# Weights, thresholds and row statistics of a ternary feed-forward stage, taken into the last batch of the attention stage before it

## The chip, the cores and the metric

One core of a Trainium2 chip runs the whole program. The metric is device time in microseconds (us) of that core, from the first to the last instruction; lower is better. The engines named below are PE (TensorE, matrix products), ACT (ScalarE), DVE (VectorE), POOL (GpSimd) and SP (SyncE, which issues the transfers). Each works through its own instructions in program order and waits on semaphores for the others.

## The reference, cut to what matters

Eight layers change a residual `x` of 4 x 512 rows of 512 numbers, four attentions and four feed-forwards in turn. The change lies at the passage from the fifth (attention, one head 512 wide) to the sixth (ternary feed-forward):

```python
x = x + _L2_attn_ref(_layernorm(x, axis=-1), ...)   # q, k with rotary turn, softmax(q k^T) v, output weight
x = x + _L2_ffn_ref(_layernorm(x, axis=-1), L2_ffn_w_fc, L2_ffn_w_proj)

def absmax_quant(x):
    gamma = jnp.max(jnp.abs(x), axis=-1, keepdims=True)
    x_hat = jnp.clip(x * Q_B / gamma, -Q_B + EPS, Q_B - EPS)
    return x_hat * gamma / Q_B
def ternarize_weights(w):
    gamma = jnp.mean(jnp.abs(w))
    return jnp.sign(jnp.round(w / (gamma + EPS))) * gamma
def bitlinear(x, w):
    xn = layer_norm(x)
    return jnp.einsum('bsd,od->bso', absmax_quant(xn), ternarize_weights(w))
h = gelu(bitlinear(x, w_fc))        # 512 -> 2048
return bitlinear(h, w_proj)         # 2048 -> 512
```

No number of the ternary first weight is known before the mean of all its magnitudes is, and no row can be turned before its mean and variance are.

## The kernel before

`build` calls the eight stages one after the other. Each stage is a block: five engine programs that start together and join at a barrier at the end, which every engine must reach before any starts the next block. The residual stays in on-chip memory (`x`, 16 tiles of 128 rows, `NT` = 16, four tiles a batch, `TT` = 4, four batches, `NB` = 4). Each stage lays its buffers over those of the stage before, from `prog.stage_at` on.

`attention512` works through a hand-written list `ORDER` of jobs (kind, batch, number), which every engine follows for its own part: `T` turns a tile of normalised rows, `qk` makes a 128-wide piece of q or k, `U` multiplies the turned rows with the joined value and output weight, `S` makes the scores of a tile of queries, `PT` turns its exponentials, and `PV` is the product that is added to `x`. `BANK` names the PSUM bank of each job.

- DVE takes row maxima (`S`, L1608), splits values into a high and a low part (`U` L1600, `PT` L1616), and adds to `x` (`PV`, L1627). In the last batch (`b + 1 == NB`), which has no next batch to prepare, it also calls `tiles_ahead` behind its first three `S` jobs: statistics of the twelve tiles of batches 0 to 2 for the next stage.
- ACT makes the exponentials and the high parts.
- POOL adds the output bias to the four tiles of a batch (L1462), prepares the next batch's inverse roots (L1440, L1442), and computes a share of a table for the last stage of the program: `TableShare` runs 31 steps a batch (16 compare-and-scale steps, L335 and L340, and 15 additions, L345), spread over the `S`, `PT` and `PV` jobs.
- SP runs `table_moves`: it fetches indices, waits for the 31 steps of a part, stores the finished part (L320), and at the end waits until the last store has landed (L323). Only then does it come to the barrier.

`ternary_feed_forward` then starts with everything: SP issues the eight transfers of the two weights (1 MB each). DVE takes the statistics of the last four tiles, POOL the inverse roots of all 16 (`roots`, L253 to L262, two of the seven steps a power), ACT the magnitudes of the four parts of the first weight. From then on:

- `row` (DVE, L1856 to L1863) normalises and clips a tile, `turn` (PE, L1975) turns it, `turned` (ACT) and `turned_rest` (DVE) split it.
- `total_of(0)` and `threshold(0)` sum the magnitudes and make the threshold; `beneath` (ACT, a sign and a relu pass) and `ternary` (DVE, L1895 and L1898) make each weight part ternary. `inner(0)` (PE, L1991) multiplies tile 0 with part after part as they come.
- `spread` (DVE, L1907 and L1911) takes the statistics of the hidden rows, POOL four small steps on them (L1773 to L1780), `centre` (ACT, L1816) and `clipped` (DVE, L1916 to L1920) normalise and clip them, and only then can `turn_hidden` (PE, L2001) go on. DVE also makes the second weight's four parts ternary here, two of them with ACT's `beneath`.

## Time and profile before

| What | Value |
|---|---|
| runs (3) | 3374.14, 3376.9, 3380.0 us; median 3376.9 |
| profiled execution, first to last instruction | 3376.4 us |
| mean granted TensorE clock over it | 0.936 |
| busy share of the span: PE, DVE, ACT, POOL | 89%, 59%, 46%, 30% |
| first products of the last attention batch's `S`, and the last `PV` product's end | 1949.8 us and 1975.5 us |
| first product of the ternary stage | 2002.6 us |
| matmuls of the ternary stage's tiles from 2060 on: PE busy in 2060 to 2100 | 35.1 of 40 us |

No time of its own is listed for the profiled execution beside its span; it lies 0.5 us under the median of the runs. A time inside the program is counted from the span's start. In the rows further down a timeline row reads: start, us of busy time, engine, line, operation, result <- sources, shapes, count; in brackets the idle time ahead of it and what ended it. `x4` with one time is four instructions merged.

### The profile page before, as it was taken

The page shows a single profiled execution, that of the slowest core. Times are in us where ns is not written, and L with a number is a line of the kernel's source. Part 1 is how long each engine was busy: PE and PEld are TensorE (multiplying, and loading weights), DVE is VectorE, ACT ScalarE, POOL GpSimd, SP SyncE. Part 2 cuts the span into 40 slices and gives each one's busy share as a digit, 9 for nine tenths or more (in the row PEclk, how much of TensorE's full clock was granted, in tenths as well). Part 3 has the DMA queues.
Part 4 walks back from the last instruction along what each step waited for, and adds up shares of the span by engine and source line. Part 5 has one row for each costly group of instructions (what it writes and reads, how often), then busy time and mean ns, then how long its engine had stood idle before and what let it go on. Part 6 is the DMA issues. An engine that isn't in the chain of part 4 may idle for free. (4 is left out here: it accounts for less than half of the span.)

```text
span 3376.4 us, 46857 instructions
## 1 busy us (share of the span) xinstructions
PE 2992.2 (89%) x16388; PEld 2260.9 (67%) x16388; DVE 1996.1 (59%) x5348; ACT 1551.2 (46%) x3598; POOL 1019.2 (30%) x1143
## 2 busy tenths in 40 slices
PE   6999799997999977978788767998689999989999
PEld 4777678885666645446566646775467777768887
DVE  5666587775555554233747767664678777742121
ACT  5777566664666652133222244444455555531000
POOL 3655333222444530000156640000133233322222
PEclk9999899998999987988899988999799999999999
DMA  2000301101000021203100020003100000020000
GB/s 87 2 2 1 113 32 32 32 32 63 1 2 1 2 67 64 100 7 117 66 4 4 2 101 1 1 1 119 34 1 1 1 1 1 1 103 13 13 13 13
DMA packets 65872, 105.51 MB, mean 31 GB/s; under 512 B 9315, under 2 KB 29795, under 8 KB 65509
## 3 DMA queue, kind: packets, MB, share of 16 engines
q1 hardware_dynamic: 65222, 102.41, 8.7%
q8 instruction: 132, 2.16, 0.3%
q14 instruction: 102, 0.84, 0.1%
q0 software_dynamic: 416, 0.10, 0.0%
HBM read 89.75 MB, written 12.85 MB: 30 GB/s over the span
## 5 line engine op out<-in xcount | busy, mean ns | idle before, releaser
L714 POOL TENSOR_SCALAR a_P<-a_P,a_rec 128x512 f32<-128x512 f32 (+3 forms) x256 | 301.5, 1190 | 350.9 <-DVE a_rec L872 350.9
L402 ACT ACTIVATE tree_value<-tree_bit,table_lut,tree_step 128x256 f32<-128x256 uint8 x496 | 275.3, 595 | 140.8 <-DVE tree_value L416 73.0
L416 DVE COPY_PREDICATED tree_value<-tree_bit,tree_value 128x256 f32<-128x256 uint8 x434 | 235.0, 547 | 133.3 <-ACT tree_value L402 104.9
L787 ACT ACTIVATE a_P<-a_P,a_low 128x384 f32<-128x384 f32 (+3 forms) x512 | 281.7, 558 | 25.0 <-DVE a_low L866 24.9
L101 PE MATMUL bank<-f_xT_hi,f_w_hi 128*128 128x512 f32 (+1 forms) x704 | 276.6, 393 | 14.0 <-DVE f_w_lo L1214 14.0
L102 PE MATMUL bank<-f_xT_hi,f_w_lo 128*128 128x512 f32 (+1 forms) x704 | 276.1, 392 | 0.0
L103 PE MATMUL bank<-f_xT_lo,f_w_hi 128*128 128x512 f32 (+1 forms) x704 | 275.7, 392 | 0.0
L1136 POOL CAST f_h_hi<-f_sg 128x512 fp32r<-128x512 f32 (+1 forms) x88 | 84.5, 961 | 587.6 <-DVE f_sg L1236 297.8
L866 DVE CUSTOM_DVE_ANT_0 a_P<-bank,a_causal 128x384 f32<-128x384 f32 (+3 forms) x512 | 222.9, 482 | 63.1 <-PE bank L949 62.6
L794 ACT ACTIVATE a_PT<-bank 128x512 f32<-128x512 f32 x320 | 174.2, 594 | 83.3 <-PE bank L960 82.6
L1236 DVE TENSOR_TENSOR f_sg<-bank,f_sg 128x512 f32<-128x512 f32 (+1 forms) x44 | 30.4, 691 | 269.4 <-PE bank L103 269.4
L960 PE MATMUL bank<-ident,a_P 128*128 128x128 f32 x1280 | 181.2, 287 | 9.2 <-issue 6.0
L960 PEld LDWEIGHTS bank<-ident,a_P 128*128 128x128 f32 x1280 | 148.9, 146 | 40.6 <-issue 30.0
L2342 ACT ACTIVATE a_PT<-bank 128x512 f32<-128x512 f32 x112 | 61.7, 595 | 220.6 <-PE bank L2615 220.6
L1172 ACT ACTIVATE f_sg<-bank 128x512 f32<-128x512 f32 (+1 forms) x44 | 26.3, 598 | 296.3 <-PE bank L103 296.2
L101 PEld LDWEIGHTS bank<-f_xT_hi,f_w_hi 128*128 128x128 f32 (+1 forms) x704 | 132.8, 189 | 43.3 <-issue 14.4
L102 PEld LDWEIGHTS bank<-f_xT_hi,f_w_lo 128*128 128x128 f32 (+1 forms) x704 | 132.8, 189 | 28.9
L103 PEld LDWEIGHTS bank<-f_xT_lo,f_w_hi 128*128 128x128 f32 (+1 forms) x704 | 132.6, 188 | 28.9
L101 PE MATMUL bank<-f_w_hi,f_h_hi 128*128 128x512 f32 (+1 forms) x352 | 140.9, 400 | 10.2 <-POOL f_h_lo L1138 10.2
L2329 ACT ACTIVATE a_P<-bank,a_nm,a_qs 128x256 f32<-128x256 f32 (+1 forms) x256 | 134.6, 545 | 22.1 <-DVE a_nm L2479 21.9
L102 PE MATMUL bank<-f_w_hi,f_h_lo 128*128 128x512 f32 (+1 forms) x352 | 138.7, 394 | 0.0
L103 PE MATMUL bank<-f_w_lo,f_h_hi 128*128 128x512 f32 (+1 forms) x352 | 138.6, 394 | 0.0
(464 smaller groups left out, 7922.7 us busy)
## 6 DMA issues: line engine op xcount, KB each, us to landing
f_w_raw<-in_f_w SPq DMA_DIRECT2D x11, 768.0 KB, 12.8
f_w_raw<-table_w SPq DMA_DIRECT2D x11, 768.0 KB, 11.2
tree_idx<-in_f_idx SPq DMA_DIRECT2D x62, 128.0 KB, 2.1
table_w<-tree_value SPq DMA_DIRECT2D x62, 128.0 KB, 1.7
x_res<-in_x SPq DMA_DIRECT2D x4, 1024.0 KB, 10.8
m_piece<-in_m_wq SPq DMA_DIRECT2D x2, 2048.0 KB, 12.1
m_piece<-in_m_wo SPq DMA_DIRECT2D x2, 2048.0 KB, 8.5
m_piece<-in_m_w_gate SPq DMA_DIRECT2D x2, 2048.0 KB, 10.4
```

Source lines behind the costliest of these rows:

```text
L101: pe.matmul(out, w[0], x[0], start=first, stop=False, skip_group_check=True)
L102: pe.matmul(out, w[1], x[0], start=False, stop=False, skip_group_check=True)
L103: return pe.matmul(out, w[0], x[1], start=False, stop=last, skip_group_check=True)
L402: act.activation(prog.tree_value[(h + to) % 4][:, :], prog.tree_bit[h % 2][0][:, :], ACT.Identity, bias=prog.table_lut[:, 2 * k:2 * k + 1] ...
L416: dve.copy_predicated(prog.tree_value[(h + keep) % 4][:, :], prog.tree_bit[h % 2][bit][:, :], prog.tree_value[(h + other) % 4][:, :]).then ...
L714: last = pool.tensor_scalar(Pr[j][:, g, col:col + n], Pr[j][:, g, col:col + n], rec[:, j, i, g:g + 1], None, ALU.mult)
L787: last = act.activation(Pr[j][:, k, col:col + n], Pr[j][:, k, col:col + n], ACT.Exp, bias=low[:, j, i, k:k + 1], scale=-1.0, accum_out=tot ...
L794: act.activation(PT[at % NPT][:, :], ps[J.bank(key)][:, :], ACT.Copy).then_inc(J.frees(key), 1)
L866: last = dve.tensor_tensor_reduce(out=Pr[j][:, k, col:col + n], in0=ps[J.bank(source)][:, col:col + n], in1=causal[:, T - n:T], scale=-sca ...
L960: last = pe.transpose(ps[J.bank(key)][:, g * P:(g + 1) * P], Pr[j][:, g, col + kt * P:col + (kt + 1) * P], prog.ident[:, :])
L1136: pool.tensor_copy(h[i % 2][0][0:n, :], sg[i % 2][0:n, :]).then_inc(c_hi.sem, 1)
L2329: e = act.activation(Pr[i][:, hh, lo:2 * P], ps[3 + j][:, h2 * 2 * P + lo:(h2 + 1) * 2 * P], ACT.Exp, bias=small["nm"][:, i, hh:hh + 1], s ...
```

## The change

- A class `TernaryMemory` lays the ternary stage's buffers by hand, at the places that the attention's last batch has done with: the first weight over q's and k's weights, the second over the joined weight and the turned rows. The two tiles of normalised rows and their turned parts lie over buffers of the `qk` jobs. The first weight is now four parts, each in one piece.
- SP issues the eight weight transfers from inside `table_moves` (`ahead`), before it waits for the last table part.
- Statistics of tiles 0 to 7 go behind the `S` jobs of batches 1 and 2, one tile each; those of tiles 8 to 11 behind the last batch's first `U` job. `tiles_ahead` is no longer called here.
- The last batch has an `ORDER` of its own with new jobs: `size` (ACT, magnitudes of a first-weight part), `row` (DVE, normalise and clip tiles 0 and 1), `fT` (turn and split them), `gamma` (sum and threshold of the first weight), `below` (ACT, the sign and relu pass of part 1).
- POOL computes the inverse roots of tiles 0 to 11 (`ternary_roots`) when it meets the first `size`, and those of tiles 12 to 15 at the start of the ternary stage.
- In the ternary stage the magnitudes of two of the second weight's parts go from DVE to ACT, and DVE takes the last four tiles' statistics behind `row(2)`.

```diff
@@ table_moves: SP @@
     for i in range(first, last):
+        if i + 1 == last:
+            ahead()
         sp.wait_ge(*prog.table_step(0, (i + 1) * TABLE_STEPS))
...
@@ ternary_roots: POOL @@
+    pool.wait_ge(*c_mv(0, done + 1))
+    for out, a, b, op in ((var[:, 0, r], prog.mv[:, r, 1], 1e-5, ALU.add), (var[:, 1, r], var[:, 0, r], half, ALU.pow),
+                          (var[:, 2, r], var[:, 1, r], var[:, 1, r], ALU.mult), (var[:, 2, r], var[:, 2, r], prog.mv[:, r, 1], ALU.mult)):
...
+    pool.tensor_tensor(var[:, 2, r], var[:, 2, r], half, ALU.pow).then_inc(prog.count("ln_pow").sem, 1)
+    pool.wait_ge(*prog.count("ln_pow")(0, done + 1))
+    pool.tensor_tensor(prog.rstd[:, r], var[:, 1, r], var[:, 2, r], ALU.mult).then_inc(c_rstd.sem, 1)
...
@@ attention512: ORDER, behind the U jobs of a batch @@
+        if b + 1 == NB:
+            ORDER += [("size", b, 0), ("S", b, 0), ("size", b, 1), ("S", b, 1), ("PT", b, 0), ("row", b, 0), ("S", b, 2), ("size", b, 2),
+                      ("PT", b, 1), ("fT", b, 0), ("PV", b, 0), ("size", b, 3), ("S", b, 3), ("row", b, 1), ("PT", b, 2), ("gamma", b, 0),
+                      ("PV", b, 1), ("fT", b, 1), ("PT", b, 3), ("PV", b, 2), ("below", b, 0), ("PV", b, 3)]
+            break
...
@@ attention512: SP @@
+            def weights_ahead():
+                for n in range(4):
+                    sp.wait_ge(*full("qk", NB - 1, 3 if n < 2 else 7))
...
+                sp.wait_ge(*full("U", NB - 1, TT - 1))
...
+            table_moves(prog, sp, *share, weights_ahead)
@@ attention512: POOL @@
             for kind, b, k in ORDER:
+                if kind == "size" and k == 0:
+                    ternary_roots(prog, pool, slice(0, HEAD_TILES), 0)
                 if kind in ("S", "PT", "PV"):
                     table.run(pool)
...
@@ attention512: ACT @@
+                elif kind == "size":
+                    act.wait_ge(*f_in[k](0, 32))
...
+                    act.activation(M.below[0][:, :, :], M.fc_part(True, k), ACT.Abs, accum_out=M.sums[:, k:k + 1]).then_inc(f_fsum.sem, 1)
...
@@ attention512: DVE, U and S @@
+                    elif k == 0 and b + 1 == NB:
+                        for t in range(HEAD_TILES - TT, HEAD_TILES):
+                            last = dve.bn_stats(prog.stats[:, t, :], x[:, t * D:(t + 1) * D])
+                        last.then_inc(f_lnstat.sem, 1)
+                    elif k == 1 and b + 1 == NB:
+                        dve.wait_ge(*f_lnstat(0, 1))
+                        for t in range(HEAD_TILES):
+                            last = dve.bn_aggr(prog.mv[:, t, :], prog.stats[:, t, :])
+                        last.then_inc(f_lnmv.sem, 1)
...
-                    if k < 3 and b + 1 == NB:
-                        tiles_ahead(prog, dve, range(k * TT, (k + 1) * TT))
+                    if b and b + 1 < NB:
+                        t = (b - 1) * TT + k
+                        dve.bn_stats(prog.stats[:, t, :], x[:, t * D:(t + 1) * D])
...
@@ ternary_feed_forward: POOL @@
-            prog.roots(pool, 1e-5, 1e-6)
+            ternary_roots(prog, pool, slice(HEAD_TILES, NT), 1)
...
@@ ternary_feed_forward: ACT @@
-            magnitudes(0)
-            magnitudes(1)
-            turned(0)
-            turned(1)
-            magnitudes(2)
-            magnitudes(3)
-            for i in range(3):
-                beneath(i)
-            gelu(0)
+            beneath(1)
+            magnitudes(0)
+            beneath(2)
+            gelu(0, (0, 1))
+            magnitudes(1)
+            gelu(0, (2, 3))
...
@@ ternary_feed_forward: DVE @@
-            prog.statistics(dve)
-            row(0)
-            row(1)
-            turned_rest(0)
-            turned_rest(1)
+            ternary("fc", 0)
+            ternary("fc", 1)
+            magnitudes(2)
+            ternary("fc", 2)
+            magnitudes(3)
+            ternary("fc", 3)
             row(2)
-            threshold(0)
-            for n in range(4):
-                ternary("fc", n)
-            magnitudes(0)
-            magnitudes(1)
+            for t in range(HEAD_TILES, NT):
+                last = dve.bn_stats(prog.stats[:, t, :], x[:, tile(0, t)])
+            last.then_inc(c_lnstat.sem, 1)
             spread(0)
-            magnitudes(2)
-            magnitudes(3)
+            dve.wait_ge(*c_lnstat(0, 2))
+            for t in range(HEAD_TILES, NT):
+                last = dve.bn_aggr(prog.mv[:, t, :], prog.stats[:, t, :])
+            last.then_inc(c_lnmv.sem, 1)
             threshold(1)
             clipped(0)
```

How the instructions stand now, at two places. POOL in the attention's last batch, before: the bias on four tiles, then straight into the 31 table steps (`table_sum`, `table_term`).

```order
L1462 TENSOR_TENSOR x_res<-x_res,a_bo 128x512 [waits xn] x4
L335 TENSOR_SCALAR table_sum_65<-table_idx_60,table_lut 128x256 [waits table_out1,table_in1]
L340 TENSOR_SCALAR table_term_62<-table_idx_60,table_lut 128x256 [waits table_step]
L340 TENSOR_SCALAR table_term_63<-table_idx_60,table_lut 128x256 [waits table_step]
L345 TENSOR_TENSOR table_sum_65<-table_sum_65,table_term_62 128x256 [waits table_step]
```

The same place in the changed kernel (`var` and `rstd` are the inverse roots of twelve tiles, `ln_mv` is DVE's signal that their means and variances are there):

```order
L1575 TENSOR_TENSOR x_res<-x_res,a_bo 128x512 [waits xn] x4
L1419 TENSOR_SCALAR var<-mv 128x12 [waits ln_mv]
L1421 TENSOR_TENSOR var<-var,mhalf 128x12 [waits ln_var]
L1421 TENSOR_TENSOR var<-var 128x12 [waits ln_var]
L1421 TENSOR_TENSOR var<-var,mv 128x12 [waits ln_var]
L1425 TENSOR_SCALAR var<-var 128x12 [waits ln_var]
L1427 TENSOR_TENSOR var<-var,mhalf 128x12 [waits ln_var]
L1429 TENSOR_TENSOR rstd<-var 128x12 [waits ln_pow]
L337 TENSOR_SCALAR table_sum_65<-table_idx_60,table_lut 128x256 [waits table_out1,table_in1]
L342 TENSOR_SCALAR table_term_62<-table_idx_60,table_lut 128x256 [waits table_step]
```

The seven root steps, and a wait for DVE ahead of them, now stand between the bias and the batch's 31 table steps.

DVE at the start of the ternary stage in the changed kernel, from the barrier to the hidden rows' statistics (`f_fc` is the ternary first weight, `f_sums` magnitudes of second-weight parts, `f_xn` a normalised tile, `f_hstats` the statistics of the hidden rows):

```order
L2016 TENSOR_SCALAR f_below_19433<-f_raw_fc,f_gamma 128x2048
L2019 SCALAR_TENSOR_TENSOR f_fc<-f_raw_fc,f_gamma,f_below_19433 128x2048 [waits h_neg]
L2019 SCALAR_TENSOR_TENSOR f_fc<-f_raw_fc,f_gamma,f_below_19431 128x2048 [waits w_below]
L2023 TENSOR_REDUCE f_sums<-f_raw_pj 128x1 [waits w_in6]
L2019 SCALAR_TENSOR_TENSOR f_fc<-f_raw_fc,f_gamma,f_below_19432 128x2048 [waits w_below]
L2023 TENSOR_REDUCE f_sums<-f_raw_pj 128x1 [waits w_in7]
L2019 SCALAR_TENSOR_TENSOR f_fc<-f_raw_fc,f_gamma,f_below_19431 128x2048 [waits w_below]
L1389 TENSOR_SCALAR f_xn_19439<-x_res,mv,rstd 128x512
...
L1396 TENSOR_SCALAR f_xn_19439<-f_xn_19439,f_gmax 128x512 [waits clip_neg]
L2062 BN_STATS stats<-x_res 128x6 x4
L2028 BN_STATS f_hstats<-f_h_19434 128x6 [waits bank_free0]
```

The block opens with the ternary first part, where before it opened with statistics, rows and the threshold; one row and four tiles' statistics follow.

## Rows read from the trace of the kernel before

**Rows 1.** Timeline of PE across the passage between the two stages.

```profile
1989.27 1.11 PE L1975 MATMUL bank<-ident,f_xn 128*128 128x128 f32 x4 [13.77 <-DVE f_xn L1863]
...
2002.62 0.77 PE L1991 MATMUL bank<-f_fc,f_xT_hi 128*128 128x512 f32 x1 [4.57 <-issue]
```

**Rows 2.** Timeline of DVE: the attention's end, the ternary stage's first rows.

```profile
1975.54 0.75 DVE L1627 SCALAR_TENSOR_TENSOR x_res<-bank,a_rec,x_res 128x512 f32<-128x512 f32 x1 [1.97 <-PE bank L103]
1976.61 2.47 DVE L209 BATCH_NORM_STATS2 stats<-x_res 128x6 f32<-128x512 f32 x4 [0.32 <-PEq L1425]
...
1987.17 0.55 DVE L1856 TENSOR_SCALAR f_xn<-x_res,mv,rstd 128x512 f32<-128x512 f32 x1 [7.68 <-POOL rstd L262]
...
1989.13 0.54 DVE L1856 TENSOR_SCALAR f_xn<-x_res,mv,rstd 128x512 f32<-128x512 f32 x1
```

**Rows 3.** Timeline of POOL: last batch's table steps, then the roots.

```profile
1939.18 2.09 POOL L335 TENSOR_SCALAR table_sum<-table_idx,table_lut 128x256 f32<-128x256 int32 x1
...
1970.37 1.55 POOL L345 TENSOR_TENSOR table_sum<-table_sum,table_term 128x256 f32<-128x256 f32 x2
1979.59 0.27 POOL L253 TENSOR_SCALAR var<-mv 128x16 f32<-128x16 f32 x1 [7.66 <-DVE mv L213]
1979.94 2.94 POOL L257 TENSOR_TENSOR var<-var,mhalf 128x16 f32<-128x16 f32 x1
```

**Rows 4.** Waits of SP's queue, 1960 to 1980: engine, line, waited for, us.

```profile
SPq L1425 <- PEq L1425: 2.3, 1, 2.3
SPq L323 <- DMA table_w<-table_sum: 1.6, 1, 1.6
```

**Rows 5.** Timeline of DVE in the last batch: `U` parts, means and variances.

```profile
1941.65 1.28 DVE L1600 TENSOR_TENSOR a_U_lo<-bank,a_U_hi 128x512 fp32r<-128x512 f32 x2
...
1955.79 0.38 DVE L495 BATCH_NORM_AGGREGATE mv<-stats 128x2 f32<-128x6 f32 x4
```

**Rows 6.** Timeline of POOL in batch 2: roots of four tiles, 31 table steps.

```profile
1873.97 1.04 POOL L1442 TENSOR_TENSOR rstd<-var,mhalf 128x4 f32<-128x4 f32 x1
1875.01 1.17 POOL L335 TENSOR_SCALAR table_sum<-table_idx,table_lut 128x256 f32<-128x256 int32 x1
...
1887.35 1.40 POOL L340 TENSOR_SCALAR table_term<-table_idx,table_lut 128x256 f32<-128x256 int32 x1
...
1905.42 1.55 POOL L345 TENSOR_TENSOR table_sum<-table_sum,table_term 128x256 f32<-128x256 f32 x2
```

**Rows 7.** Timeline of DVE in batch 2: four normalised tiles beside those steps.

```profile
1887.29 2.62 DVE L1546 TENSOR_SCALAR a_xn<-x_res,mv,rstd 128x512 f32<-128x512 f32 x4
```

**Rows 8.** Waits of DVE in batches 1 and 2: line, waited for, us, times, longest.

```profile
DVE a_nm L1608 <- PE bank L103: 10.5, 8, 2.0
```

**Rows 9.** The last batch in one stretch: length, then busy PE, PEld, DVE, ACT, POOL, clock.

```profile
1943.00:1976.00 33.00, 30.82 (x136) 24.77 (x134) 17.63 (x42) 6.38 (x14) 26.70 (x29) 0.95 0.02 5
```

**Rows 10.** Timeline of DVE: ternary parts, magnitudes, hidden rows' statistics, first clip.

```profile
1998.85 1.29 DVE L1895 TENSOR_SCALAR f_below<-f_raw_fc,f_gamma 128x2048 f32<-128x2048 f32 x1
2000.17 2.35 DVE L1898 SCALAR_TENSOR_TENSOR f_fc<-f_raw_fc,f_gamma,f_below 128x2048 fp32r<-128x2048 f32 x1
...
2010.50 2.35 DVE L1898 SCALAR_TENSOR_TENSOR f_fc<-f_raw_fc,f_gamma,f_below 128x2048 fp32r<-128x2048 f32 x1 [1.49 <-ACT f_below L1805]
2012.77 4.47 DVE L1902 TENSOR_REDUCE f_sums<-f_raw_pj 128x1 f32<-128x2048 f32 x2
2017.16 2.46 DVE L1907 BATCH_NORM_STATS2 f_hstats<-f_h 128x6 f32<-128x512 f32 x4
...
2025.76 2.29 DVE L1916 TENSOR_REDUCE f_hmax<-f_h 128x1 f32<-128x2048 f32 x1 [0.20 <-ACT f_h L1816]
```

**Rows 11.** Timeline of POOL: the four steps on the first hidden rows' statistics.

```profile
2020.22 0.23 POOL L1773 TENSOR_SCALAR f_hvar<-f_hmv 128x1 f32<-128x1 f32 x1 [33.08 <-DVE f_hmv L1911]
...
2021.58 0.25 POOL L1780 TENSOR_SCALAR f_hshift<-f_hvar 128x1 f32<-128x1 f32 x1 [0.19 <-POOL f_hvar L1777]
```

**Rows 12.** Timeline of ACT: the first hidden rows normalised (`centre`).

```profile
2023.57 2.08 ACT L1816 ACTIVATE f_h<-f_h,f_hshift,f_hrstd 128x2048 f32<-128x2048 f32 x1
```

More of the change, by code:

```diff
@@ L303, in table_part, with table_moves @@
     return part[:, i % 2 * TABLE_COLS:(i % 2 + 1) * TABLE_COLS]
-def table_moves(prog, sp, first, last):
+def table_moves(prog, sp, first, last, ahead):
     def fetch(i):
@@ new lines, in ternary_roots @@
+def ternary_roots(prog, pool, r, done):
+    c_mv, c_var, c_rstd = prog.count("ln_mv"), prog.count("ln_var"), prog.count("ln_rstd")
+    var, half = prog.var, prog.mhalf[:, r]
+    steps = 5 * done
+    pool.wait_ge(*c_mv(0, done + 1))
+    for out, a, b, op in ((var[:, 0, r], prog.mv[:, r, 1], 1e-5, ALU.add), (var[:, 1, r], var[:, 0, r], half, ALU.pow),
+                          (var[:, 2, r], var[:, 1, r], var[:, 1, r], ALU.mult), (var[:, 2, r], var[:, 2, r], prog.mv[:, r, 1], ALU.mult)):
+        if op == ALU.add:
+            last = pool.tensor_scalar(out, a, b, None, op)
+        else:
+            last = pool.tensor_tensor(out, a, b, op)
+        steps += 1
+        last.then_inc(c_var.sem, 1)
+        pool.wait_ge(*c_var(0, steps))
+    pool.tensor_scalar(var[:, 2, r], var[:, 2, r], 1e-6, None, ALU.add).then_inc(c_var.sem, 1)
+    pool.wait_ge(*c_var(0, steps + 1))
+    pool.tensor_tensor(var[:, 2, r], var[:, 2, r], half, ALU.pow).then_inc(prog.count("ln_pow").sem, 1)
+    pool.wait_ge(*prog.count("ln_pow")(0, done + 1))
+    pool.tensor_tensor(prog.rstd[:, r], var[:, 1, r], var[:, 2, r], ALU.mult).then_inc(c_rstd.sem, 1)
@@ L1417, in attention512 @@
     c_uhi, c_max, c_pthi, c_rec = (prog.count(n) for n in ("u_hi", "row_max", "pt_hi", "rec"))
+    f_in = [prog.count(f"w_in{i}") for i in range(8)]
+    f_fsum, f_below, f_sign, f_xhi, f_xn = (prog.count(n) for n in ("w_sums", "w_below", "w_sign", "fT_hi", "xn_ready"))
+    f_gamma, f_rstd, f_lnstat, f_lnmv = (prog.count(n) for n in ("w_gamma", "ln_rstd", "ln_stats", "ln_mv"))
     NQK = len(QK)
@@ L1633, in _ @@
                 key = (kind, b, k)
-                if kind == "T":
+                if kind in ("size", "row", "below"):
+                    continue
+                if kind == "fT":
+                    pe.wait_ge(*f_xn(0, k + 1))
+                    pe.wait_ge(*vacant(*key))
+                    for c in range(DC):
+                        last = pe.transpose(bank(*key)[:, c * P:(c + 1) * P], M.xn[k][:, c * P:(c + 1) * P], prog.ident[:, :])
+                elif kind == "gamma":
+                    pe.wait_ge(*f_fsum(0, 4))
+                    pe.wait_ge(*vacant(*key))
+                    last = pe.matmul(bank(*key)[:, 0:4], prog.ones[:, :], M.sums[:, 0:4], start=True, stop=True)
+                elif kind == "T":
                     pe.wait_ge(*c_xn(0, b * TT + k + 1))
@@ L1736, in ternary_feed_forward @@
     h_norm, h_max, h_neg, h_ready, h_hi = (prog.count(n) for n in ("h_norm", "h_max", "h_neg", "h_ready", "h_hi"))
-    once = [prog.count(n) for n in ("ln_stats", "ln_mv", "ln_rstd")]
-    c_var = prog.count("ln_var")
+    c_lnstat, c_lnmv, c_rstd, c_var, c_pow = (prog.count(n) for n in ("ln_stats", "ln_mv", "ln_rstd", "ln_var", "ln_pow"))
     H_BANK = (4, 5, 6, 4)
-    jobs = [(("T", 0), 5), (("T", 1), 5), (("sum", 0), 7)] + [(("F", 0, n), n) for n in range(4)]
+    jobs = [(("F", 0, n), n) for n in range(4)]
     for t in range(NT):
@@ L1805, in beneath, with gelu @@
                 act.activation(below[i % 2][:, :, :], below[i % 2][:, :, :], ACT.Relu).then_inc(c_below.sem, 1)
-            def gelu(t):
+            def gelu(t, which=range(4)):
                 if t >= 2:
                     act.wait_ge(*full("H", t - 2, 3))
-                for n in range(4):
+                for n in which:
                     act.wait_ge(*full("F", t, n))
@@ L1990, in inner @@
                         for i in (0, 1):
-                            last = pe.matmul(ps[n][:, :], xT[t % 2][i][:, k, :], fc[:, k, n * D:(n + 1) * D], start=k == 0 and i == 0,
+                            last = pe.matmul(ps[n][:, :], xT[t % 2][i][:, k, :], fc[:, n, k, :], start=k == 0 and i == 0,
                                              stop=k == DC - 1 and i == 1)
```

168 lines of the change are left out of this document (106 added, 62 removed).

## The prediction

> **What bounds the kernel now.** I read the timeline of PE first, since PE is the busiest engine, and looked for the hole that the change aims at. Between the attention's last product at 1975.5 and the first product of the ternary stage at 2002.62, PE does only two tiles' turns: it waits 13.77 us for a normalised tile and later 4.57 us for the first ternary part [rows 1]. DVE's timeline says what fills the hole [rows 2]: its last addition to `x` ends at 1976.29, the barrier takes 0.32 us, four tiles' statistics follow, then 7.68 us of waiting for POOL's roots, then rows at 1.96 us each (1987.17 to 1989.13). Behind the hole the weight parts come at ACT's pace, 2.35 us of DVE and 1.49 us of waiting each, the last one done at 2012.85 [rows 10]. Then come magnitudes, hidden statistics, and at 2025.76 the first `clipped`.
>
> That instruction is my yardstick. All that DVE, ACT, PE and POOL do from it on is in the same order in both kernels, and it waits for the hidden rows' normalisation, so whatever moves it moves the end of the program by as much. The sum is made on the profiled execution (3376.4 us, 0.5 under the median of the runs).
>
> **POOL and the barrier, the term that decides.** In the last batch POOL runs its table steps from 1939.18 to 1971.92 (1970.37 + 1.55) without a break [rows 3], and was done 4.4 us before the attention was. The change puts roots ahead of these 31 steps, and a wait for DVE ahead of the roots. Step by step:
>
> - DVE begins the first `U` part at 1941.65 as before, 0.64 us (half of 1.28): 1942.3. Four statistics, 2.46 us by the four like ones at 2017.16 [rows 10]: 1944.75. The second `U` part, 0.64: 1945.4. Twelve aggregations at 0.095 (0.38 for four [rows 5]), 1.14: signal at 1946.5. PE does not mind: it needs that second part only for the fourth `U` product, after its third.
> - The roots of 16 tiles took 7.55 us (1979.59 to the row that they release at 1987.17). Two of the seven steps are powers, 2.94 us at 16 columns [rows 3] and 1.04 at four [rows 6]: 0.158 a column, so 2.31 at twelve. 7.55 - 2 x 0.63 = 6.3 us; with the signal's 0.1, ready at 1952.9. Upper bound: the whole 7.55.
> - The 31 steps took 31.96 us in batch 2 (1875.01 to 1906.97 [rows 6]) and 32.74 in the last batch. I take 31.96, because the longer one began beside DVE's last q and k work, which is over by now: POOL ends at 1984.9.
> - SP may store the part only then. Before, it waited 1.6 us for the landing and another 2.3 at the barrier [rows 4], which opened about 1976.4: it arrived at 1974.1, 2.2 us after POOL's last step. Now 1987.1. With the barrier's 0.32, the ternary stage begins at **1987.4**, 10.8 us later than before.
>
> **The last batch's other engines** are not what ends last. ACT gains four magnitude passes, a sign and relu pair and two copies, about 13 us (a pair is the 2.35 + 1.49 = 3.84 us of ACT's pace above, a pass taken as half of it); it was busy 6.38 of 33 us [rows 9]. Two of the passes stand between a score and what PE waits for next. DVE loses three groups of statistics and gets two rows. Walking through the order with these durations I get the last addition at about 1980. Bounds: 1976.3 with all of it hidden, 1989.1 with every added pass on the path, which would cost 2 us beyond POOL. Below 1987.1 it costs nothing.
>
> **Batches 1 and 2** get eight statistics of 0.62 us, behind row maxima. DVE waits 10.5 us in eight of these places for PE's next scores [rows 8], so I count nothing; with all of it on the path, 4.9 us. **The eight transfers** move ahead of SP's last wait. They wait for `qk` and `U`, over by 1950, and nothing is queued behind them but the table store, 35 us later. I count nothing.
>
> **The ternary stage, from its start s = 1987.4 to `clipped`**, with start-to-start distances of [rows 10]: the compare 1.32, each ternary pass 2.27, each magnitude pass 2.2. Passes of parts 0 and 1, a magnitude, part 2, a magnitude, part 3: the last begins at s + 12.5 and ends at s + 14.85. ACT's pairs for parts 2 and 3, with one magnitude pass between, need at most 3 x 3.84 = 11.5, so DVE does not wait for them. Then one row, 1.96, and four statistics, 2.4: `spread` begins at s + 19.15. From its start to POOL's first step was 3.06 us (2017.16 to 2020.22 [rows 11]); now four aggregations lie between, 0.38: s + 22.6.
>
> Here is the second price on POOL: the roots of tiles 12 to 15 stand ahead of the hidden rows' four steps. At four columns they take 7.55 - 2 x 1.90 = 3.75 us: s + 26.35. The four steps took 1.61 (2020.22 to 2021.83), so s + 27.95, and from `centre` to `clipped` it was 2.19 (2023.57 [rows 12] to 2025.76): s + 30.15. The other way to `centre`, over tile 1's products and their gelu, took 10.7 us from the last ternary part (2012.85 to 2023.57), which now gives s + 25.6. POOL comes 2.3 us later than that, so slower products up to that amount would not show.
>
> **Sum:** 1987.4 + 30.15 = 2017.55 instead of 2025.76, 8.2 us earlier. The median of the runs less this is 3376.9 - 8.2 = **3368.7 us**. Of some 17.6 us that the move would give with POOL out of the way, POOL takes 7.1 at the barrier and 2.3 behind it.
>
> **A rule against it.** In [rows 6, 7] DVE normalises four tiles beside the table steps: one POOL step takes 1.40 instead of 1.17, and the batch's 31.96 us hold that. In the last batch the two rows have four such DVE operations, so the term already has their price. The Trainium skill (SBUF — State Buffer, "Who interferes with whom") says that GpSimd and a VectorE operation of this kind take a shared port by turns, and that the later one blocks fully. By it each of the four could hold POOL for its own 0.55 us, 2.2 in all, and the sum would be nearer 3370.5; the 0.23 of the row is less than that.
>
> **Rivals.**
>
> 1. *The rows collide with POOL in full.* POOL's first step of the last batch took 2.09 us beside DVE's q and k work, 0.92 more than the 1.17 of batch 2 [rows 3, 6]. Four of these are 3.7 us, some 3.3 beyond what is in the term: 8.2 - 3.3 = 4.9 us gained, 3372.0 us, which is no change by my bound. For it: that step. Against it: the 0.23 beside just such DVE operations.
> 2. *The hole closes entirely.* Were POOL and SP no later than the batch's own end at 1980, the stage would start 7.1 us earlier: 15.3 us gained, 3361.6 us. It needs POOL's 31 steps to end by 1977.5. Against it: POOL's order is fixed, and its steps lie without gaps in [rows 3, 6]; nothing makes them shorter.
> 3. *Slower than before.* DVE's, ACT's and the transfers' added work in the last batch stretches POOL's steps one and all by the 0.92 of that first step: 28.5 us, 3397 us. The gain is gone from 9 such steps of 31, and from 17 (15.6 us) the kernel is measurably slower. For it: POOL is now on the path, so each such us counts. Against it: POOL kept its pace in batch 2 while DVE, ACT and PE worked beside it.
>
> **How the numbers follow.** A difference of 0.2%, 6.75 us, is about what a measurement of this kernel can tell from no change. Forecast as worked out, with its terms a little off: 0.71. First rival: 0.13. Second: 0.06. Third: 0.06. The remaining 0.04 is a gain of 2 to 6 us from small losses, such as the eight statistics of batches 1 and 2. The forecast's own range comes from roots at 6.3 to 7.55, table steps at 31.7 (without the 0.23) to 32.74, 0.4 either way at the barrier, 2 us if ACT's passes lie on the path, and 1.5 us of spread between the runs: 3366 to 3372.5. Since 0.71 alone is too little, the range takes in the first rival and a part of the second's side: 3363.5 to 3373.5. The forecast lies 1.45 us beyond the 0.2% line, so about a tenth of its chance falls within it: faster 0.64 + 0.06 = 0.70; the same 0.07 + 0.13 + 0.04 = 0.24; slower 0.06.
>
> **What will show it.** In the changed profile POOL's twelve-column roots should begin near 1946.5 and its last table addition end near 1985; DVE's first compare should follow near 1987.4, with DVE, PE and ACT idle from about 1980 until then and SP the last at the barrier. The first ternary product should start some 3.7 us behind that, four-column roots near 2010, and `clipped` near 2017.5. I am wrong in the main term if POOL ends before the batch's last addition, if DVE's or ACT's last work of the batch is the later one, or if the products of batches 1 and 2 have already shifted when the last batch begins.

## The result

The changed kernel takes 3362.64 us (median; runs from 3358.44 to 3365.48) beside 3377.14 us of the kernel before on the same chip: 14.5 us less. The ratio is 0.995, with a 95% interval of 0.9938 to 0.9962, which is a gain of 13 to 21 us. The forecast was 8.2 us and 3368.7 us, and its range ended at 3363.5: the direction was right, the gain nearly twice what was forecast. The profiled execution spans 3358.3 us, 18.1 us less than the one before.

Four instructions cut the program into pieces that can be compared: DVE's first `U` part of the last batch, the first product with the ternary first weight, DVE's first `clipped` (the yardstick), and the last product of the ternary stage. All times in the table are differences of their starts in the timelines, in us.

| Stretch | before | changed | changed, second profile | difference |
|---|---|---|---|---|
| program start to first `U` part | 1941.65 | 1940.40 | 1942.43 | (not touched) |
| `U` part to first product | 60.97 | 48.68 | 48.64 | -12.29 |
| first product to `clipped` | 23.14 | 26.15 | 26.13 | +3.01 |
| `clipped` to the ternary stage's last product | 293.78 | 287.99 | 288.03 | **-5.79** |

The second profile is that of the run "a_again" below. The stretches that hold the change repeat within 0.04 us in these two profiles, and within 0.3 us in a third, a_sink below, whose edit lies in another stage. The stages ahead, which no kernel here alters, do not: over the thirteen profiles of this study the first `U` part starts anywhere from 1937.5 to 1944.2. So a profile's whole span tells changes of a few us badly, and I compare stretches.

The passage that the forecast modelled, `U` part to `clipped`, gained 12.29 - 3.01 = 9.28 us. Another 5.79 us came from behind the yardstick, where the forecast had said nothing would happen. Together 15.1 us; the other 3 of the 18.1 lie in stages that the change doesn't touch (1.25 ahead, 1.8 behind).

### The profile page after: what moved, and what is told of

It reads as the page before. It is cut to its first block and busy times, and to the rows that moved or that the text cites. A ratio compares the mean times of both kernels' runs of the same rounds, so it can differ in the third digit from the quotient of the medians.

```text
span 3358.3 us, 46872 instructions
## 1 busy us (share of the span) xinstructions
PE 2978.5 (89%) x16388; PEld 2255.5 (67%) x16388; DVE 1990.4 (59%) x5346; ACT 1554.5 (46%) x3602; POOL 1020.2 (30%) x1150
## 5 line engine op out<-in xcount | busy, mean ns | idle before, releaser
L101 PE MATMUL bank<-f_xT_hi,f_w_hi 128*128 128x512 f32 (+1 forms) x704 | 275.5, 391 | 14.5 <-DVE f_w_lo L1216 14.5
```

Source lines behind the costliest of these rows:

```text
L101: pe.matmul(out, w[0], x[0], start=first, stop=False, skip_group_check=True)
```

## The profile after

POOL's timeline in the changed kernel, from the wait for DVE's means to the hidden rows' last step; it answers to [rows 3, 6, 11]:

```profile
1944.97 0.27 POOL L1419 TENSOR_SCALAR var<-mv 128x12 f32<-128x12 f32 x1 [7.02 <-DVE mv L1739]
1945.31 2.30 POOL L1421 TENSOR_TENSOR var<-var,mhalf 128x12 f32<-128x12 f32 x1
...
1951.21 1.17 POOL L337 TENSOR_SCALAR table_sum<-table_idx,table_lut 128x256 f32<-128x256 int32 x1
...
1957.37 1.19 POOL L342 TENSOR_SCALAR table_term<-table_idx,table_lut 128x256 f32<-128x256 int32 x1
1958.65 0.98 POOL L347 TENSOR_TENSOR table_sum<-table_sum,table_term 128x256 f32<-128x256 f32 x1
...
1981.58 1.52 POOL L347 TENSOR_TENSOR table_sum<-table_sum,table_term 128x256 f32<-128x256 f32 x2
2007.65 0.24 POOL L1419 TENSOR_SCALAR var<-mv 128x4 f32<-128x4 f32 x1 [24.55 <-DVE mv L2067]
...
2011.38 0.23 POOL L1909 TENSOR_SCALAR f_hvar<-f_hmv 128x1 f32<-128x1 f32 x1
...
2012.74 0.25 POOL L1916 TENSOR_SCALAR f_hshift<-f_hvar 128x1 f32<-128x1 f32 x1 [0.20 <-POOL f_hvar L1913]
```

Seven us of waiting, 6.24 us of roots, 31.89 us of table steps, done at 1983.10. The waits of SP's queue around the end of the attention (engine and line, waited for, us), which answer to [rows 4], show that SP came to the barrier last, and that nobody kept it waiting there (0.2 us):

```profile
SPq L325 <- DMA table_w<-table_sum: 1.4, 1, 1.4
SPq L1525 <- PEq L1525: 0.2, 1, 0.2
```

DVE's timeline answers to [rows 2, 5, 10]: the last batch's start, its last addition to `x`, 9.56 us of waiting at the barrier, and the ternary stage to `clipped`:

```profile
1940.40 0.68 DVE L1729 TENSOR_TENSOR a_U_lo<-bank,a_U_hi 128x512 fp32r<-128x512 f32 x1
...
1975.05 0.75 DVE L1779 SCALAR_TENSOR_TENSOR x_res<-bank,a_rec,x_res 128x512 f32<-128x512 f32 x1 [1.97 <-PE bank L103]
1985.36 1.28 DVE L2016 TENSOR_SCALAR f_below<-f_raw_fc,f_gamma 128x2048 f32<-128x2048 f32 x1 [9.56 <-PEq L1525]
...
1997.86 2.34 DVE L2019 SCALAR_TENSOR_TENSOR f_fc<-f_raw_fc,f_gamma,f_below 128x2048 fp32r<-128x2048 f32 x1
...
2004.45 2.46 DVE L2028 BATCH_NORM_STATS2 f_hstats<-f_h 128x6 f32<-128x512 f32 x4
...
2015.23 2.29 DVE L2037 TENSOR_REDUCE f_hmax<-f_h 128x1 f32<-128x2048 f32 x1 [4.19 <-ACT f_h L1951]
```

ACT's row ahead of `clipped` answers to [rows 12]; ACT waited for POOL:

```profile
2013.03 2.09 ACT L1951 ACTIVATE f_h<-f_h,f_hshift,f_hrstd 128x2048 f32<-128x2048 f32 x1 [2.14 <-POOL f_hshift L1916]
```

Where the 5.79 us came from shows in PE's timeline in the middle of the ternary stage. First the kernel before, then the changed one (start, length, what). In both the last row is the 24th product behind the first, with nothing but such products between:

```profile
2160.13 0.39 PE L1991 MATMUL bank<-f_fc,f_xT_hi 128*128 128x512 f32 x1
2160.36 0.39 PE L1991 MATMUL bank<-f_fc,f_xT_lo 128*128 128x512 f32 x1
...
2165.73 0.39 PE L2012 MATMUL bank<-f_pj,f_hT_hi 128*128 128x512 f32 x1
```

```profile
2147.03 0.39 PE L2114 MATMUL bank<-f_fc,f_xT_lo 128*128 128x512 f32 x1
2147.26 0.39 PE L2114 MATMUL bank<-f_fc,f_xT_hi 128*128 128x512 f32 x1
...
2152.47 0.39 PE L2114 MATMUL bank<-f_fc,f_xT_lo 128*128 128x512 f32 x1
```

24 products take 5.60 us before and 5.44 after: 233.3 and 226.7 ns from start to start. The mean over the stage, where the granted clock is 1.00, is 233.3 ns before, for both weights, and 227.6 ns (first weight) and 226.9 ns (second) after. From the fifth tile's first product to the stage's last one the clock is 1.00 all along. These are that stretch's rows, before and after (length, then busy time and count of PE, PEld, DVE, ACT, POOL, then the clock, and the transfers' share and rate):

```profile
2085.51:2319.53 234.02, 225.88 (x1082) 181.78 (x1081) 151.72 (x225) 93.38 (x124) 15.80 (x50) 1.00 0.00 1
```

```profile
2074.21:2303.22 229.01, 220.88 (x1082) 182.18 (x1081) 151.59 (x225) 93.41 (x124) 15.83 (x50) 1.00 0.00 1
```

The same 1082 products and turns take 5.01 us less, the greater part of the 5.79. From `clipped` to the fourth tile's first product nothing is gained (40.10 and 40.11 us). The other 0.78 us lie in the passage between, from the fourth tile's first product to the fifth's, in which PE has its lower clock for a part of the time:

```profile
2065.86:2085.51 19.65, 19.02 (x86) 15.28 (x85) 12.14 (x18) 7.54 (x11) 1.21 (x4) 0.92 0.00 1
```

```profile
2055.34:2074.21 18.87, 18.24 (x86) 14.96 (x85) 12.13 (x18) 7.54 (x11) 1.21 (x4) 0.94 0.00 1
```

Of the stage's 1024 such products 896 come behind the fourth tile's first one, where PE is the bound, so some 6 ns of each is 5.4 us. PE's work, its order and the other engines' work beside it are the same there. What differs is where the buffers lie. In both kernels the streamed weights begin at bytes 51904 and 84672 of each partition, 192 modulo 512. The turned rows that PE loads (`xT`, `hT`) began at 142080 and 170752 before, 256 modulo 512, because the two small buffers `gamma` and `sums` (64 bytes) stand ahead of them; `TernaryMemory` puts them at 199360 and 158400, 192 modulo 512. The distance was 64 and is now 0.

## Experiments

"Distance" is always the address of the loaded operand less that of the streamed one, in bytes modulo 512.

**1. The addresses alone, in the kernel before (b_addr).**

```diff
-    gamma = prog.sb(name + "_gamma", [P, 8], F32)
-    sums = prog.sb(name + "_sums", [P, 8], F32)
     below = [prog.sb(f"{name}_below{i}", [P, 4, D], F32) for i in range(3)]
...
     hshift = prog.sb(name + "_hshift", [P, 1], F32)
+    gamma = prog.sb(name + "_gamma", [P, 8], F32)
+    sums = prog.sb(name + "_sums", [P, 8], F32)
```

> The kernel before with one thing changed: the two small buffers gamma and sums (64 bytes together) are allocated behind the ternary stage's other buffers, so that the turned rows (the weights that PE loads, xT and hT) lie 64 bytes lower. Nothing is moved in time. Theory A (addresses): a float32r product of 512 columns takes 233.3 ns from start to start where the loaded and the streamed operand lie 64 bytes apart modulo 512, and 226.7 to 228 ns where they lie 0 apart, as in the changed kernel; expected: the 1024 products of the ternary stage at about 227 ns, that stage 5.5 to 6.5 us shorter, the program 3371 us instead of 3377, the ternary stage's first product and first clipped where they were. Theory L (layout of the first weight in four contiguous parts): no change, 233 ns, 3377 us. Theory T (the earlier start or other work beside the products): no change, 233 ns, 3377 us.

Measured: 3375.0 us beside 3380.0 us, ratio 0.999 (0.9979 to 1.0001): 5 us by the medians, but an interval that reaches no change. The stretches are sharper: `U` part to `clipped` 83.97 us (84.11 before), `clipped` to the last product 288.46 instead of 293.78. PE's timeline in the middle of the stage:

```profile
2160.11 0.39 PE L1991 MATMUL bank<-f_fc,f_xT_hi 128*128 128x512 f32 x1
2160.34 0.39 PE L1991 MATMUL bank<-f_fc,f_xT_lo 128*128 128x512 f32 x1
...
2165.55 0.39 PE L2012 MATMUL bank<-f_pj,f_hT_hi 128*128 128x512 f32 x1
```

5.44 us for 24, as in the changed kernel; 227.7 and 226.9 ns in the mean of the stage. Moving 64 bytes brings 5.3 of the 5.8 us, with nothing moved in time; I had expected 5.5 to 6.5. The steady stretch from the fifth tile on takes 229.01 us, exactly that of the changed kernel. The passage ahead of it takes 19.35 us at a mean clock of 0.91, where the changed kernel has 18.87 at 0.94: the missing 0.5 us goes with the clock and not with the addresses. The edit also moves `below`, `xn` and `h` by 64 bytes. In s_small, further down, these lie as in the kernel before modulo 512, and the products with `hT` are fast all the same.

**2. The layout alone (b_parts).**

```diff
-    fc = prog.sb(name + "_fc", [P, DC, 4 * D], F32R)
+    fc = prog.sb(name + "_fc", [P, 4, DC, D], F32R)
...
-    last = pe.matmul(ps[n][:, :], xT[t % 2][i][:, k, :], fc[:, k, n * D:(n + 1) * D], ...
+    last = pe.matmul(ps[n][:, :], xT[t % 2][i][:, k, :], fc[:, n, k, :], ...
```

> The kernel before with the first weight stored as four contiguous parts, as the change stores it; all addresses of buffers as before, so the operands still lie 64 bytes apart modulo 512. Theory A (addresses): 233.3 ns for both weights' products, no change. Theory L (layout): the first weight's 512 products at 227 ns, about 3 us less; the second weight's, whose layout is the same in both kernels, at 233 ns, which would leave the gain in them unexplained.

Measured: 233.3 ns for both weights, `clipped` to the last product 293.79 us, 3379.9 us in one run. The layout does nothing.

**3. The addresses undone in the changed kernel (a_shift).**

```diff
+        at += 64
         self.hT = [prog.sb(f"{name}_hT_{n}", ...
...
-        at = FLAT_AT
+        at = FLAT_AT - 64
         self.xn = [prog.sb(f"{name}_xn{i}", ...
```

> The changed kernel with its turned rows moved: xn and xT 64 bytes down (448 instead of 0 apart modulo 512 from the first weight), hT 64 bytes up (64 apart, as in the kernel before). Nothing is moved in time. Theory A (addresses): products at about 233 ns again, the ternary stage 5.5 to 6.5 us longer, the program about 3368.5 us, which is 8 to 9 us under the kernel before, the passage's gain alone. Theories L (layout) and T (time or neighbours): 227 ns as in the changed kernel, 3362.6 us.

Measured: 3366.5 us, ratio 0.9962 (0.995 to 0.9974). `U` part to `clipped` is as in the changed kernel (74.76 us, 74.83 there), `clipped` to the last product 291.67 us, 3.7 longer (5.5 to 6.5 expected). The second weight's products, at distance 64, take 233.4 ns again; the first weight's, at 448, take 229.3, which I had expected to be slow in full. PE's timeline, first weight and then second, the last row of each pair the 24th product behind its first (5.50 and 5.60 us):

```profile
2145.30 0.39 PE L2115 MATMUL bank<-f_fc,f_xT_lo 128*128 128x512 f32 x1
...
2150.80 0.39 PE L2115 MATMUL bank<-f_fc,f_xT_lo 128*128 128x512 f32 x1
2151.49 0.40 PE L2136 MATMUL bank<-f_pj,f_hT_hi 128*128 128x512 f32 x1
...
2157.09 0.40 PE L2136 MATMUL bank<-f_pj,f_hT_hi 128*128 128x512 f32 x1
```

**4. Other distances, and other places (s_small, s_moved).** Both are the kernel before with the ternary stage's buffers placed by hand. The edits in s_small, and behind them those in s_moved:

```diff
+    prog.at = near(57) + 32      # xT of even tiles; near(k) is stage_at + 2048 k
+    prog.at = near(60) + 128     # xT of odd tiles
+    prog.at = near(63) + 256     # hT
...
+    at = prog.stage_at + 64                   # first weight
+    at = prog.stage_at + 16 * D * 4 + 64      # second weight
+    prog.at = near(57) + 64
+    prog.at = near(60) + 0
+    prog.at = near(63) + 256
```

> The kernel before with the ternary stage's turned rows at other distances from the weights that are streamed past them (modulo 512; 64 before): even tiles' xT 32, odd tiles' xT 128, hT 256. If 0 alone is fast: 229 to 233.5 ns in all three. If distances of whole 128 or 256 bytes are free: 227 ns for the odd tiles, or for hT. If only the loaded operand's own place matters (192 modulo 512 fast): slow in all three.

> The kernel before with both weights of the ternary stage 64 bytes higher (256 instead of 192 modulo 512), and xT of even tiles at a distance of 0 from them, of odd tiles at 448, hT at 192. Theory A (the distance between the operands counts): even tiles' products 227 to 228 ns, odd tiles' 229 to 230, hT's about 232 ns. Rival (the loaded operand's own place counts, 192 modulo 512 fast): even tiles (at 256) 233 ns, odd tiles (at 192) 227 ns.

Measured in one run each, mean from start to start: distance 32, 233.4 ns; 128, 232.9; 256, 227.3 (s_small); 0, with both operands moved by 64, 227.4; 448, 229.2; 192, 229.0 (s_moved), the last faster than I had expected. From s_small, 24 products of even tiles (distance 32, 5.60 us) and 15 with `hT` (256, 3.40 us):

```profile
2158.78 0.40 PE L1997 MATMUL bank<-f_fc,f_xT_lo 128*128 128x512 f32 x1
...
2164.38 0.40 PE L1997 MATMUL bank<-f_fc,f_xT_lo 128*128 128x512 f32 x1
2166.47 0.39 PE L2018 MATMUL bank<-f_pj,f_hT_hi 128*128 128x512 f32 x1
...
2169.87 0.39 PE L2018 MATMUL bank<-f_pj,f_hT_lo 128*128 128x512 f32 x1
```

From s_moved, 24 products of even tiles with both operands at 256 (distance 0, 5.44 us):

```profile
2157.68 0.39 PE L1997 MATMUL bank<-f_fc,f_xT_hi 128*128 128x512 f32 x1
...
2163.12 0.39 PE L1997 MATMUL bank<-f_fc,f_xT_hi 128*128 128x512 f32 x1
```

The distance counts and not the place: both operands at 256 are as fast as both at 192. And 0 is not the only fast distance. With 64 from the kernel before, the values are 227 to 228 ns at 0 and 256, 229 at 192 and 448, 233 at 32, 64 and 128: all of it fits a distance taken modulo 256, though 320, for one, was not measured. `clipped` to the last product follows: 290.76 us (s_small) and 289.73 us (s_moved).

**5. The same in another stage (a_sink).** The window attention's float32r products lie at distances 128 and 384, in both kernels.

```diff
+    sink = prog.sb(name + "_sink", [P, 2, H], F32)
     wc, wc_raw = prog.pair(name + "_wc", [P, DC, P])
...
-    sink = prog.sb(name + "_sink", [P, 2, H], F32)
```

> The changed kernel with one thing changed in the window attention, a stage that the change does not touch: the buffer sink (128 bytes) stands ahead of that stage's weights instead of between them and its other buffers, so that loaded and streamed operands of its float32r products lie 0 apart modulo 512 (128 and 384 before). Theory A (addresses): these 1008 products go from 232.6 to about 227 ns, the stage 4 to 5.6 us shorter, the program 3357 to 3358.5 us instead of 3362.6. Rival (the distance matters only in the ternary stage's pattern of one streamed piece under two loaded ones): 232.6 ns as before, no change.

Measured: 3359.8 us, ratio 0.9942 (0.9927 to 0.9957), which overlaps the changed kernel's. PE's timeline in the window attention, the changed kernel and then a_sink, each time from one product to the eleventh behind it (2.55 and 2.50 us):

```profile
2505.47 0.39 PE L101 MATMUL bank<-a_w_hi,a_OT_hi 128*128 128x512 f32 x1
...
2508.02 0.40 PE L103 MATMUL bank<-a_w_lo,a_OT_hi 128*128 128x512 f32 x1
```

```profile
2502.57 0.40 PE L101 MATMUL bank<-a_w_hi,a_OT_hi 128*128 128x512 f32 x1
...
2505.07 0.39 PE L103 MATMUL bank<-a_w_lo,a_OT_hi 128*128 128x512 f32 x1
```

The 768 products with `OT` go from 232.6 to 227.9 ns, as the distance says; the 192 with `compT`, now also at distance 0, only from 232.2 to 231.9. These come three at a time between other kinds of products; whether that is the reason is not shown. The stage, from its first `OT` product to the first product of the next, takes 533.2 us where the changed kernel's two profiles have 534.7 and 535.0. That would be 1.5 to 1.8 us, where 4 to 5.6 had been expected; but a_hidden_first below, without this edit, shows 533.4. Over all thirteen profiles the two with this edit (a_sink, a_all) have 533.2 and 533.4, ten of the eleven without it 534.6 to 536.0. So the products' gain is shown, some 1.5 us for the stage is likely, and one for the program is not shown.

**6. POOL's order in the last batch (a_table_first).**

```diff
                 if kind == "size" and k == 0:
+                    for _ in range(3):
+                        table.run(pool)
                     ternary_roots(prog, pool, slice(0, HEAD_TILES), 0)
                 if kind in ("S", "PT", "PV"):
-                    table.run(pool)
+                    if table.n < 3 * NT:
+                        table.run(pool)
```

> The changed kernel with three of the last batch's twelve calls of the table share, 7 of its 31 steps, put on POOL ahead of the twelve-column roots, into the 7.0 us in which POOL waits for DVE there. Theory of the prediction (POOL's table steps and the store behind them are what ends last at the barrier): roots 0 to 1 us later, POOL's last table addition near 1976.5 instead of 1983.1, the ternary stage 6 to 7 us earlier, and the program as much: 3356 us instead of 3362.6. Rival (the batch's own work, ACT's passes or the weight transfers, ends just under POOL): POOL ends 6 to 7 us earlier, but the stage starts at most 3 us earlier, with another engine named at the barrier, 3360 us or more. Second rival: the rows and PE's turns wait longer for later roots, and the last addition to x moves up by as much as POOL is earlier: no change.

Measured: 3356.5 us, ratio 0.9928 (0.9913 to 0.9943). POOL's timeline and then DVE's first row of the ternary stage:

```profile
1945.10 1.15 POOL L342 TENSOR_SCALAR table_term<-table_idx,table_lut 128x256 f32<-128x256 int32 x1
1946.33 0.26 POOL L1419 TENSOR_SCALAR var<-mv 128x12 f32<-128x12 f32 x1
...
1975.58 1.52 POOL L347 TENSOR_TENSOR table_sum<-table_sum,table_term 128x256 f32<-128x256 f32 x2
1979.36 1.29 DVE L2019 TENSOR_SCALAR f_below<-f_raw_fc,f_gamma 128x2048 f32<-128x2048 f32 x1 [3.40 <-PEq L1525]
```

POOL ends at 1977.10, 6.0 us earlier, and the stage starts 6.0 us earlier; `U` part to first product is 42.82 us (48.68). POOL, with SP's store behind it, did set the start.

**7. The second price on POOL (a_hidden_first).**

```diff
-            ternary_roots(prog, pool, slice(HEAD_TILES, NT), 1)
             for t in range(NT):
...
                 pool.tensor_scalar(hshift[:, :], hvar[:, :], -1.0, None, ALU.mult).then_inc(h_rstd.sem, 1)
+                if t == 0:
+                    ternary_roots(prog, pool, slice(HEAD_TILES, NT), 1)
```

> The changed kernel with POOL's roots of tiles 12 to 15 put behind its four steps on the first hidden rows, instead of ahead of them. Theory of the prediction (the roots are a second price on POOL, 2.3 us, after which the other way to centre, over tile 1's products and gelu, ends last): POOL's hidden steps 3.7 us earlier, ACT's centre only about 2.1 us earlier, since ACT ends gelu of tile 1 2.14 us before centre in the changed profile; clipped 2.1 us earlier and the program 3360.5 us instead of 3362.6. Rival (ACT or PE hold centre anyway, or POOL's roots now collide with DVE's clipped): less than 1 us.

Measured: 3362.5 us, ratio 0.9952 (0.9935 to 0.9969), no difference that runs can tell from the changed kernel. In this profile the first `U` part came 3.8 us later than in the changed kernel's, in stages that both share, which hides the gain. The stretches show it: first product to `clipped` 23.86 us instead of 26.15. POOL's timeline and ACT's:

```profile
2011.23 0.24 POOL L1908 TENSOR_SCALAR f_hvar<-f_hmv 128x1 f32<-128x1 f32 x1 [24.41 <-DVE f_hmv L2033]
2012.93 0.24 POOL L1419 TENSOR_SCALAR var<-mv 128x4 f32<-128x4 f32 x1
2013.89 0.69 ACT L1948 ACTIVATE f_h<-bank,f_gamma 128x512 f32<-128x512 f32 x1 [1.12 <-PE bank L2115]
2014.48 2.08 ACT L1952 ACTIVATE f_h<-f_h,f_hshift,f_hrstd 128x2048 f32<-128x2048 f32 x1
```

POOL's `f_hshift` is there at 2012.9 now; ACT goes to `centre` without a wait behind its last gelu. The bound has passed to PE's products and the gelu, 2.29 us earlier.

**8. Three edits together (a_best, a_all, beside a_again).** a_best holds the edits of 6 and 7 and a third one, with which SP no longer waits at the barrier for its last store:

```diff
@@ table_moves @@
-    for i in (last - 2, last - 1):
-        sp.wait_ge(*prog.table_out[i % 2](0, 16 * (i // 2 + 1)))
+    i = last - 2
+    sp.wait_ge(*prog.table_out[i % 2](0, 16 * (i // 2 + 1)))
@@ ternary_feed_forward @@
+        @block.sync
+        def _(sp):
+            sp.wait_ge(*prog.table_out[3 % 2](0, 16 * (3 // 2 + 1)))
```

a_all has the edit of 5 as well; a_again is the changed kernel once more.

> The changed kernel with three edits on POOL and SP together: 7 table steps ahead of the twelve-column roots, the hidden rows' steps ahead of the four-column roots, and SP's wait for the landing of the last table part taken out of the attention's block and put into the ternary stage's. Theory of the prediction (POOL, then SP's store and landing, set the start of the ternary stage; roots delay the hidden rows): against the changed kernel the stage starts 5.9 us earlier by the first edit and 1.5 to 2 us by the third, since POOL's end (35.4 to 36.8 us after the last batch's first U part) is then the last thing at the barrier, close to the batch's own end (35.7 us after it); clipped comes another 2.3 us earlier by the second. In all 9.7 to 10.5 us less than the changed kernel, about 3352 us, 25 us under the kernel before. Rival (the third edit buys nothing, because POOL's or SP's last store is still waited for at the barrier, or the last attention addition is later): 8 us less, 3354.5 us.

> The kernel with the three edits, and the buffer sink of the window attention moved as well, so that this stage's operands lie 0 apart too. By the products alone (227 instead of 232.6 ns, 1008 of them) 4 to 5.6 us less than without it. By what the run with that edit alone showed (median start to start 227 ns, mean 230 to 231, no shorter stage than the spread of about 1 us between runs): 0 to 2 us less.

> The changed kernel itself, unaltered, on the chip of the two versions above, so that they are compared with it at the same place. Expected 3362 to 3364 us; from the last batch's first U part to the first F product 48.7 us, from there to clipped 26.1 us, and from there to the ternary stage's last product 288 us, all within 0.4 us, whatever the stages ahead do.

Measured on one chip: a_again 3364.3 us, ratio 0.9953 (0.994 to 0.9965); a_best 3354.2 us, 0.9932 (0.9918 to 0.9945); a_all 3349.6 us, 0.9912 (0.9898 to 0.9925). By the runs' medians a_best is 10.1 us under a_again; by the profiles, from the `U` part to the stage's last product, 7.5 (355.27 and 362.81), which I trust more, and which is less than I had expected. `U` part to first product fell to 41.39 us, 1.43 less than with the table steps alone, so the third edit works. But first product to `clipped` is 25.34 and not 23.86: most of edit 7's gain is gone. Two rows of stretches say why (length, then busy time and count of PE, PEld, DVE, ACT, POOL, then the granted clock, 0.50 and 1.00), the last part's products of tile 0 in a_best and in a_hidden_first:

```profile
1993.80:1997.00 3.20, 3.16 (x8) 2.51 (x9) 3.10 (x7) 0.17 (x1) 0.00 (x0) 0.50 0.00 0
```

```profile
2003.90:2006.00 2.10, 2.02 (x9) 1.50 (x10) 2.00 (x6) 0.20 (x1) 0.00 (x0) 1.00 0.00 0
```

Each comes behind the same 2.35 us of waiting for DVE; in a_best PE's clock fell to its lower level (1.2 GHz) behind that wait, and the eight products took 3.45 us to the next turn instead of 1.96. That is the missing 1.5 us. Another 1.2 us lies behind `clipped` (288.54 us, 287.35 in a_hidden_first). The steady stretch from the fifth tile on is as long in both (228.95 and 229.06). Of the 1.2 us 0.8 lie in the passage ahead of it, again with the lower mean clock in a_best (first row):

```profile
2048.14:2067.59 19.45, 18.82 (x87) 15.34 (x85) 12.14 (x18) 7.54 (x11) 1.22 (x4) 0.91 0.01 1
```

```profile
2056.33:2074.95 18.62, 17.99 (x87) 14.76 (x85) 12.14 (x18) 7.54 (x11) 1.22 (x4) 0.95 0.01 1
```

The remaining 0.5 us lie between `clipped` and the fourth tile (40.13 and 39.66 us), at the same mean clock of 0.76; their cause stays open.

a_all is the fastest kernel measured, though its interval overlaps a_best's. Of the 4.5 us between the two profiles 3.7 lie ahead of the last batch's first `U` part, in code that both share, and 1.5 in the window attention; 0.7 is lost again elsewhere. Whether edit 5 helps stays open.

## Why the prediction was wrong

Point by point, the modelled passage first, times from the `U` part or from the stage's start s:

- *Signal of the means*: 4.57 us behind the `U` part; forecast 4.95. Twelve aggregations took 0.90, not 1.14.
- *Roots of twelve columns*: 6.24 us; forecast 6.3. A power took 2.30; forecast 2.31. (The sixteen columns that this was scaled from took 7.58 us by the rows, not 7.55, which changes nothing.)
- *Table steps*: 31.89 us; forecast 31.96.
- *Store, landing and barrier*: 2.26 us; forecast 2.5.
- *The batch's own end*: 35.4 us behind the `U` part (1975.80); forecast some 38.3 (about 1980). It cost nothing, since it lay below POOL's end.
- *Statistics of batches 1 and 2*: batch 0's first `U` part to the last batch's takes 218.19 us, 218.20 before. Nothing, as counted.
- *The ternary stage to `clipped`*: last ternary part at s + 12.50 (forecast 12.5), `spread` at s + 19.09 (19.15), POOL at s + 22.29 (22.6), the roots 3.73 to the next step (3.75), `clipped` at s + 29.87 (30.15). ACT's last gelu ended at s + 25.53 (25.6 for the other way to `centre`), and a_hidden_first shows that this way was next, by 2.29 us (2.3).

These terms sum to 9.28 us where 8.2 was forecast; the error of 1.1 is spread over five of them.

**The step that failed** is the sentence on the yardstick: "whatever moves it moves the end of the program by as much". It put what lies behind the yardstick at nothing, and the runs show 5.79 us there. With the passage's 9.28 us alone the forecast's own subtraction would have given 3367.6 us. The sentence was argued from the order of the instructions, which is the same. But the change also moves buffers, and the 960 products behind the yardstick depend on where their operands lie: 5.3 us by b_addr. The other 0.5 us goes with PE's clock in the passage ahead of the fifth tile. It is no accident of one profile (18.94 us there in a_again, 18.87 in the first), but the order of the instructions doesn't show it either.

The addresses stand in the diff, and the pace stood in the trace of before. There the ternary stage's products take 233 ns; those of the attention beside it, of the same shape and at distance 0, take 227 ns once the clock is 1.00 (the second row is the 15th product behind the first, 3.40 us):

```profile
1946.36 0.39 PE L101 MATMUL bank<-a_wvo_hi,a_xT_hi 128*128 128x512 f32 x1
...
1949.76 0.39 PE L101 MATMUL bank<-a_KT_hi,a_QT_hi 128*128 128x512 f32 x1
```

I read the stage's busy share (35.1 of 40 us) and not its pace.

**The rivals.** The first (rows collide with POOL in full, 3.7 us) is refuted: beside DVE's first row one step took 1.19 and one addition 0.98 instead of 0.74, beside its second one step 1.19 instead of 1.15, 0.3 us in all. The rule of the Trainium skill weighed there (SBUF — State Buffer, "Who interferes with whom") would have made it 2.2. The third (all steps stretched) did not happen. The second, the hole closed entirely, forecast 3361.6 us, nearer to the measured time than the forecast itself. It is wrong all the same: POOL ended at 1983.10 and DVE waited 9.56 us at the barrier. The time alone would have confirmed a mechanism that was not there.

## What to carry to other kernels

When a change lays out buffers anew, compare the pace of the products (start to start, same shape, same clock) and the address of each product's loaded operand with that of its streamed one, before and after: two small buffers of 64 bytes together, laid in between, cost 5.3 us here. Forecast a passage against marks on both sides of it, and test a sentence like "from here on all is the same" on the steady part too. Where stages ahead vary by several us from run to run, judge an edit by the stretch that holds it, and do not add the gains of edits that shift PE's pauses: the clock may take some back.

## What the runs showed of the hardware

- A float32r product of 128 x 128 by 512 columns, each with a load of its own, at a granted clock of 1.00 (2.4 GHz): in the ternary stage, 226.7 to 228 ns where the operands' distance is 0 or 256, 229 at 192 and 448, 233 at 32, 64 and 128. One kind of product in the window attention stayed at 231.9 at distance 0. Why the distance counts is not settled. The Trainium skill (TensorE: Matmul & The Clock Gate, "Step-by-step: what each phase is for") says that loading the next weights takes nothing from the running product, since PE reads the two through ports of their own; by that one would not expect the distance to matter. Here it does, and the measurement decides.
- Behind 2.35 us without work PE's granted clock was 1.00 in one kernel (a_hidden_first) and 0.50 (1.2 GHz) in another (a_best) with the same instructions on PE. Edits that only shift the work ahead can change that: 1.5 us here, and 0.8 us in a passage further on.
